# Gated expert outputs added into the towers' input by accumulating DMAs instead of GpSimd additions

## What is computed

```python
h = relu(einsum('bi,eio->beo', x, eW1) + eb1)            # 8 experts, 1024 -> 1024
h = relu(einsum('beh,eho->beo', h, eW2) + eb2)           # 1024 -> 512
expert_out = einsum('beh,eho->beo', h, eW3) + eb3        # 512 -> 256
gates = softmax(einsum('bi,tie->bte', x, gW) + gb, axis=-1)   # 2 tasks, 8 gates each
tin = einsum('bte,bed->btd', gates, expert_out)          # gated sum over the experts
th = relu(einsum('btd,tdh->bth', tin, tW1) + tb1)        # towers: 256 -> 512
th = relu(einsum('bth,tho->bto', th, tW2) + tb2)         # 512 -> 256
out = sigmoid(einsum('bth,tho->bto', th, tW3) + tb3)     # 256 -> 1
```

## Time and profile before

| | us |
|---|---|
| median of three runs | 585.0 |
| the profiled execution | 584.63 |
| its span | 582.9 |
| PE busy | 575.5 |
| DVE busy | 464.5 |
| ACT busy | 265.2 |
| POOL busy | 44.2 |

### The profile page before, as it was taken

One profiled execution on the slowest core, in us unless ns is written; L12 is line 12 of the kernel. 1 busy time (PEld: TensorE's weight loads), 2 busy tenths in 40 slices (PEclk: granted clock), 3 DMA queues, 4 the chain that ended last, 5 costly groups with the idle time before them and its releaser, 6 DMA issues.

```text
span 582.9 us, 9215 instructions
## 1 busy us (share of the span) xinstructions
PE 575.5 (99%) x3315; PEld 505.0 (87%) x3315; DVE 464.5 (80%) x591; ACT 265.2 (46%) x336; POOL 44.2 (8%) x46
## 2 busy tenths in 40 slices
PE   9999999999999999999999999999999999999998
PEld 6888888888999889988999889998899889998776
DVE  7954199895998859996799859987698959988492
ACT  3545175333654264441745255451644336543553
POOL 0000010012000300003000300003000120004000
PEclk9999999999999999999999999999999999999999
DMA  8340334225223422316122432315141252235100
GB/s 310 134 144 12 133 112 143 75 65 224 72 72 108 179 73 94 122 36 252 48 96 72 158 130 72 115 65 187 65 144 72 70 218 72 72 118 170 36 0 2
DMA packets 23277, 63.27 MB, mean 109 GB/s; under 512 B 1617, under 2 KB 6865, under 8 KB 19682
## 3 DMA queue, kind: packets, MB, share of 16 engines
q1 hardware_dynamic: 21906, 58.64, 28.4%
q0 software_dynamic: 1216, 4.23, 2.2%
q10 hardware_dynamic: 144, 0.26, 0.1%
HBM read 63.08 MB, written 0.04 MB: 108 GB/s over the span
## 4 chain that ended last, share of the span: by engine, by line
PE 92%; DVE 4%; issue 2%; ACT 1%; DVEq 0%; ACTq 0%
PE psum L277 24%; PE psum L279 24%; PE psum L278 24%; PE psum L418 12%; PE psum L420 6%; DVE w_lo L780 1%; DVE scratch L816 1%; PE psum L501 1%; PE psum L375 1%; DVE h_lo L791 0%; PE psum L478 0%; PE psum L477 0%; DVE scratch L822 0%; DVE scratch L868 0%; ACT w_hi L735 0%
## 5 line engine op out<-in xcount | busy, mean ns | idle before, releaser
L277 PE MATMUL psum<-h_hi,w_hi 128*128 128x512 f32 (+1 forms) x340 | 131.9, 388 | 0.8 <-DVE h_lo L791 0.8
L278 PE MATMUL psum<-h_lo,w_hi 128*128 128x512 f32 (+1 forms) x340 | 131.7, 387 | 0.0
L279 PE MATMUL psum<-h_hi,w_lo 128*128 128x512 f32 (+1 forms) x340 | 131.7, 387 | 0.0
L780 DVE TENSOR_TENSOR w_lo<-w_raw,w_hi 128x1024 fp32r<-128x1024 f32 (+1 forms) x79 | 111.2, 1427 | 10.5 <-ACT w_hi L588 8.1
L791 DVE SCALAR_TENSOR_TENSOR h_lo<-scratch,h_hi 128x512 fp32r<-128x512 f32 (+1 forms) x68 | 61.7, 910 | 47.1 <-ACT scratch L673 34.9
L277 PE MATMUL psum<-t_both,w_hi 128*128 128x256 f32 x336 | 95.4, 284 | 1.6 <-DVE scratch L874 1.6
L279 PE MATMUL psum<-t_both,w_lo 128*128 128x256 f32 x336 | 95.2, 283 | 0.0
L278 PE MATMUL psum<-t_both,w_hi 128*128 128x256 f32 x336 | 95.1, 283 | 0.0
L619 ACT ACTIVATE w_hi<-w_raw 128x1536 fp32r<-128x1536 f32 x28 | 41.8, 1494 | 80.7 <-PE psum L279 39.5
L277 PEld LDWEIGHTS psum<-h_hi,w_hi 128*128 128x128 f32 x340 | 63.9, 188 | 14.0 <-DVE h_lo L791 1.2
L279 PEld LDWEIGHTS psum<-h_hi,w_lo 128*128 128x128 f32 x340 | 63.9, 188 | 13.0
(11 more groups left out here) (104 smaller groups left out, 807.7 us busy)
## 6 DMA issues: line engine op xcount, KB each, us to landing
w_raw<-eW_pairs SPq DMA_DIRECT2D x28, 1024.0 KB, 4.8
w_raw<-eW SPq DMA_DIRECT2D x40, 512.0 KB, 3.7
scratch<-gates_dram POOLq DMA_DIRECT2D x8, 512.0 KB, 3.9
w_raw<-eW_first SPq DMA_DIRECT2D x7, 512.0 KB, 6.2
w_raw<-tW SPq DMA_DIRECT2D x4, 512.0 KB, 3.6
scratch<-xT SPq DMA_DIRECT2D x7, 256.0 KB, 6.2
w_raw<-eW_first SPq DMA_DIRECT2D x2, 256.0 KB, 4.0
scratch<-xT ACTq DMA_DIRECT2D x1, 256.0 KB, 3.3
```

What stands on the lines that cost most here:

```text
L277: pe.matmul(bank, weights_hi, moving_hi, start=first, stop=False)
L278: pe.matmul(bank, weights_hi, moving_lo, start=False, stop=False)
L279: return pe.matmul(bank, weights_lo, moving_hi, start=False, stop=last)
L780: dve.tensor_tensor(wide(w_lo, slots), raw, wide(w_hi, slots).bitcast(F32), ALU.subtract).then_inc(slot_ready, 1)
```

## The change

The additions on POOL are replaced by DMAs issued by POOL that add their source to their destination (`accum_op`), both in SBUF, 128 x 512 floats each. POOL waits for each to land before it issues the next, and the gates' DMA follows the fourth. `added` is split in `zeroed_in`, for the zeroing, and `poured`, for the DMAs. POOL's loop is written out in Python.

The gated products get four slots: two in `gated` as before, and slots 2 and 3 of `sums`. DVE doesn't wait for POOL between them any more; before the third it waits for the splits of the last pair's sums. In turn `sum2` of a pass's first pair waits for `gates_landed`, which comes after the four DMAs of the pass before.

```diff
+        def gated_slot(n):
+            return gated[:, n, :] if n < 2 else sums[:, n, :]
...
             def sum2(e, i):
 
+                if i == 0:
+
+                    dve.wait_ge(gates_landed, e * DMA)
                 dve.wait_ge(summed, 3 * PAIRS * (e - 1) + 3 * i + 1)
...
                         n = o * T + t
 
-                        dve.wait_ge(added, GATED * (done - 1) + n + 1)
-                        dve.scalar_tensor_tensor(gated[:, n % 2, :], banks[BANK_OUT3[o]][:],
+                        if n == 2:
+                            dve.wait_ge(slot_ready, splits(done) + 3 * PAIRS)
+                        dve.scalar_tensor_tensor(gated_slot(n), banks[BANK_OUT3[o]][:],
...
-            dve.wait_ge(added, GATED * (E - 1) + 2)
+            dve.wait_ge(poured, DMA * GATED * (E - 1))
             dve.wait_ge(gates_landed, E * DMA)
...
-                pool.memset(task_in[:, n * OUT3:(n + 1) * OUT3, :], 0.0).then_inc(added, 1)
+                pool.memset(task_in[:, n * OUT3:(n + 1) * OUT3, :], 0.0).then_inc(zeroed_in, 1)
...
-            pool.wait_ge(added, 2)
-            with pool.Fori(1, E) as e:
+            pool.wait_ge(zeroed_in, T)
+            for e in range(1, E):
                 for o in range(OUT3):
                     for t in range(T):
                         n = o * T + t
                         pool.wait_ge(gated_ready, GATED * (e - 1) + n + 2)
-                        pool.tensor_tensor(task_in[:, t * OUT3 + o, :], task_in[:, t * OUT3 + o, :],
-                                           gated[:, n % 2, :], ALU.add).then_inc(added, 1)
+                        pool.dma_start(task_in[:, t * OUT3 + o, :], gated_slot(n), accum_op=ALU.add) \
+                            .then_inc(poured, DMA)
+
+                        pool.wait_ge(poured, DMA * (GATED * (e - 1) + n + 1))
                 pool.dma_start(gates[:], gates_dram[one(e)].rearrange("e t b -> (e t) b").partition_broadcast(P)) \
                     .then_inc(gates_landed, DMA)
```

More of the change, by code:

```diff
@@ L220, in moe_towers @@
         gated_ready = sem("gated_ready")
-        added = sem("added")
+        zeroed_in = sem("zeroed_in")
+        poured = sem("poured")
         zeroed = sem("zeroed")
```

## The result

The changed kernel takes 663.25 us (median of four runs, 663.06 to 663.81) against 584.99 us: 1.134 of the time before, interval 1.132 to 1.136. That is slower, as forecast, and inside the range of 604 to 670, but 30 us above the forecast's 633: the loss is 78 us where 48 were expected. The profiled execution's span went from 582.9 to 662.0 us, by 79.1.

What follows compares the result with a forecast made beforehand. The prediction took PE to bound the loop. It added 6.3 us before pass 1 and 41.8 us at six boundaries, 48.1 in all, to 584.6 us for 632.7, forecast 633 us, range 604 to 670.

Steps and rivals of the forecast that it cites:

- PE-bound, with no idle after pass 1, and nothing to win from POOL's additions: Whole loop: PE busy 575.5 of 582.9 us, so removing POOL's 28 additions (35 us) is worth nothing by itself.
- DVE's 9.02 us from sum2 to the second sum31: DVE at a pass's start: running through without a break, as seen in pass 1, it needs 9.02 us between these.
- The first boundary, 6.3 us: Before pass 1: sum2 waits for the first gates' broadcast, landing at 80.07 instead of starting at 73.80; nothing covers 6.27 us.
- T = 3.8 us for each of the four: POOL's accumulating DMAs at each boundary: time from one issue to the next; loss per boundary 4T - 8.2, 7.0 us.
- the first two of a boundary share the engines with two weight loads: Reason for T nearer the broadcast's 4.1 us: 1 MB loads there take 5.7 us to land instead of 4.8.
- All lateness but 0.35 us: Pairs 0 to 2 of a pass: DVE, running without a break, hands on its lateness to PE except 0.35 us.
- Where PE's lateness shows: Passes 2 to 7: 4.4 us of PE idle before a pass, some 2.6 us per pass waiting for L874.
- The clock's rival: Rival: slower clock after each of seven stalls, 1.4 us each, 10 us in all, giving 643 us; chance 0.07.
- The tail: Ahead of the towers: last gates land by 552.0 us against tail_gate's start at 553.29, so no cost, covered by 1.3 us.
- The Trainium skill's fit: GpSimd DMA as 2.0 us plus bytes at 436 GB/s: 2.6 us to landing, T = 2.9, 611 us; not used uncorrected.

Runs made afterwards that it cites:

- loads after the first DMA: The changed kernel, but SyncE issues a pass's weight loads only when the first accumulating DMA has landed: 665.18 us.
- loads last: The changed kernel, but SyncE issues the weight loads of passes 2 to 7 only when all four accumulating DMAs have landed: 659.62 us.
- kept busy: The changed kernel with 28 matmuls on zeros put into PE's idle time before each pass: 663.49 us.
- mark: The changed kernel, but sum2 waits for a one-column memset by POOL after the fourth DMA (and once ahead of the loop), not for the gates: 634.21 us.
- plain copy: The changed kernel with the same 28 DMAs without accum_op, copying the gated product over the sum: 639.86 us.
- in flight: The changed kernel, but POOL issues an expert's four accumulating DMAs without waiting between them, then waits for all before the gates' DMA: 624.15 us.
- kernel with the additions on POOL: The changed kernel with its slots and its wait in sum2, but the additions made by POOL again: 590.75 us.
- own slots: The changed kernel with four slots of their own for the gated products, so sum2 needs no wait for gates_landed; accumulating DMAs stay: 584.68 us, 0.9997 of the kernel before.

## Why the prediction was right in kind, and where it was short

**The formula.** All these kernels obey one line. Let x be the time from the first DMA to sum2. The second sum31 comes 9.02 us after sum2, and the next pass's first gated product reaches POOL 46.55 us after that (214.53 - 167.98 in the changed kernel), so that a pass takes x + 55.6 us. The constant is read from the changed kernel; the others test it.

| kernel | x before pass 2 | x + 55.57 | to the next boundary, measured |
|---|---|---|---|
| changed | 23.53 | 79.10 | 79.10 |
| loads after the first DMA | 23.65 | 79.22 | 79.22 |
| loads last | 22.87 | 78.44 | 78.45 |
| kept busy | 23.04 | 78.61 | 78.61 |
| mark | 19.54 | 75.11 | 75.13 |
| plain copy | 19.42 | 74.99 | 75.00 |
| in flight | 16.93 | 72.50 | 72.52 |

Each entry is a difference of starts in POOL's and DVE's timelines, as shown above for the changed kernel. With PE as the bound a pass took 67.0 us, so by an estimate from this line DVE is unnoticed up to x = 11.4. The kernel with the additions on POOL has x = 143.88 - 134.71 = 9.2 and loses nothing there; no run lies between that and 16.9.

**Point by point.**

- PE-bound, with no idle after pass 1, and nothing to win from POOL's additions: right (own slots: 0.9997).
- DVE's 9.02 us from sum2 to the second sum31: right, to the hundredth.
- The first boundary, 6.3 us: right in its mechanism, while the exact agreement with the 6.3 in POOL's starts is luck. DVE is 79.56 - 73.80 = 5.8 us late at sum2, because the broadcast landed in 3.9 us instead of 4.6. The other 0.5 us lie between the first gated product and POOL: its addition began 129.17 - 128.34 = 0.8 us after the product's start, its DMA 135.43 - 134.10 = 1.3 us.
- T = 3.8 us for each of the four: this is the term that was mis-sized. Three took 3.6, one 8.9; the mean is 4.9, near the upper end of the forecast's 2.6 to 5.1. The first alone is 8.9 - 3.8 = 5.1 us over, 31 us in six boundaries, which is the whole miss. The step that failed in its working is "the first two of a boundary share the engines with two weight loads": I had seen the sharing and taken from the loads' 5.7 against 4.8 us that it costs about a microsecond. But that is what a transfer of 1 MB loses beside another. The small one, issued after both, landed last: just before 144.21, 8.5 us after its issue. The first load had landed by 139.77, and the second took 8.4 us. The price should have been bounded by the time of everything in flight ahead of it.
- Against it stand the three others, 0.24 us shorter each, 4 us in six boundaries.
- "All lateness but 0.35 us": the loss is lateness plus 0.2, another 0.5 us per boundary or 3 in all. The 0.35 read from pass 1 against pass 2 was no slack: from the second sum31 to POOL's next addition both took 46.35 us (129.17 - 82.82, and 195.91 - 149.56), so what is late at the second sum31 is late at the boundary in full; PE's start merely stood 0.35 us differently to it. The 0.2 (46.55 against 46.35) is again POOL's start: before pass 3 its DMA begins 214.53 - 213.49 = 1.04 us after the first gated product, where its addition began 195.91 - 195.08 = 0.83 us after it. DVE itself takes 45.5 us from the second sum31 to that product in both kernels.
- The sum of these, 31 - 4 + 3 us, and 0.1 to 0.2 us per boundary for gates that landed later, gives 31 of the 31 us missing in the span.
- Where PE's lateness shows: in part wrong. Forecast were 4.4 us of idle before a pass and 2.6 us per pass of waiting for L874 (L882 now). Before pass 2 the idle is 9.6 us, more because the lateness is, but the waits for L882 come to 1.9 us in the whole span. In their place PE was busy for longer, at the slow clock: 69.43 us in pass 2 (below, the number after the comma) instead of 67.09.

```profile
162.10:241.20 79.10, 69.43 (x408) 61.85 (x408) 54.97 (x70) 30.59 (x38) 4.05 (x5) 0.93 0.35 106
```

- The clock's rival: the fall happens (0.50 after each stall), which I gave little weight, and its cost is hidden for the reason given there. Its price of 10 us was also too low: PE's busy time rose by 591.3 - 575.5 = 15.8 us, and the first four matmuls after a stall took 2.07 us instead of 1.07, 0.25 each where 0.15 was put in. Showing that it is hidden took the kernel that kept PE busy.
- The tail: no cost. The first DMA there took 5.9 us, the four 16.6 to the gates' issue at 627.43. The slowest of the kernel's broadcasts behind the four DMAs landed in 4.2 us, so the gates were there by 631.6 at the latest, and the product that needs them, tail_gate, starts at 632.37 without a wait.
- The Trainium skill's fit ("DMA: Bandwidth & Descriptors", Anatomy of one DMA — SWDGE (gpsimd) path) gives an estimate of 2.6 us to landing for 256 KB. In this case's traces the plain copy landed in 2.3 us in the median, the accumulating one in 3.3. So the fit is near for copying and too low for adding, and it has no term for sharing, which decided here.

## What to carry to other kernels

A wait put on an in-order engine is priced by everything queued behind it, and the free time is that of the most urgent of these: here DVE could be held until about 11.4 us after the first DMA's issue and was held until 23.5. Reusing a buffer moves a consumer's release into a producer's path; 1 KB more of memory on each partition and a buffer that was dead anyway made the same DMAs free. And price a small DMA at what is in flight ahead of it, not at its median landing: look at its place in time among the large loads, one by one.

## What the runs showed of the hardware

- An accumulating DMA of 128 x 512 floats within SBUF, issued by GpSimd: 3.6 us from one issue to the next when each is waited for, a plain copy 2.6. The engine is occupied 0.87 us by issuing it, against 0.54.
- Beside one load of 1 MB issued just before it, 7.1 to 7.5 us; beside two, 8.7 to 9.5 over all kernels that waited for each. Four in flight together beside two loads: 12.8 to 13.2 us for all.
- In each of PE's seven idle times of 6 to 10 us the granted clock fell to 0.50 (1.2 GHz), and it was back at 1.00 only 3 to 6 us after the restart. With 28 matmuls in each idle time it stayed at 1.00 around four starts of a pass and fell to 0.50 shortly before the three others.
